# Attention block on one core: the two v of a pair made alternately in two PSUM banks

## The reference

```python
h = group_norm(x, scale, bias)                      # 32 groups
q, k, v = split(h @ qkv_w + qkv_b, 3, axis=-1)
q, k, v = (a.reshape(batch * 8, 1024, 64) for a in (q, k, v))
weight = softmax(einsum('btc,bsc->bts', q / 64**.25, k / 64**.25))
a = einsum('bts,bsc->btc', weight, v).reshape(batch, 1024, 512)
out = x + a @ proj_w + proj_b
```

## Time and profile before

| | |
|---|---|
| median of three runs | 3357.51 us |
| the profiled execution | 3357.48 us |
| its span, first to last instruction | 3355.7 us |
| PE busy | 3289.6 us, 98% |
| DVE busy | 2895.4 us, 86% |
| ACT busy | 2010.0 us, 60% |
| POOL busy | 1656.2 us, 49% |
| mean granted clock of PE | 0.997 |

### The profile page before, as it was taken

How to read it: one execution, slowest core, us unless ns; L and a number is a source line. 1 busy time by engine, 2 the same in 40 slices (tenths; PEclk the granted TensorE clock), 3 DMA queues, 4 the chain that set the end, 5 groups by cost and what they waited for, 6 DMA issues and landing times.

```text
span 3355.7 us, 66951 instructions
## 1 busy us (share of the span) xinstructions
PE 3289.6 (98%) x24128; PEld 2483.9 (74%) x24128; DVE 2895.4 (86%) x3601; ACT 2010.0 (60%) x3857; POOL 1656.2 (49%) x2762
## 2 busy tenths in 40 slices
PE   4999999999999999999999999999999999999998
PEld 4777777777777777777777777777777777777775
DVE  6888888888888888888888888888888888888886
ACT  4665665665665656656656666566566566565663
POOL 3454554554545544545545455445455454554452
PEclk9999999999999999999999999999999999999999
DMA  5888888888878888888888787878888788887777
GB/s 124 197 195 196 198 193 196 194 198 192 199 195 196 195 195 197 196 193 197 196 193 198 193 199 190 199 196 196 196 194 198 191 198 195 198 193 189 185 190 179
DMA packets 312633, 646.84 MB, mean 193 GB/s; under 512 B 80624, under 2 KB 146160, under 8 KB 312304
## 3 DMA queue, kind: packets, MB, share of 16 engines
q1 hardware_dynamic: 270784, 573.87, 72.6%
q10 hardware_dynamic: 41520, 68.71, 7.2%
HBM read 71.84 MB, written 33.55 MB: 31 GB/s over the span
## 4 chain that ended last, share of the span: by engine, by line
PE 94%; DVE 2%; SPq 1%; ACT 1%; DMA 0%; POOL 0%; issue 0%; ACTq 0%; POOLq 0%
PE pv_ps L372 25%; PE s_ps L343 23%; PE c_ps L408 7%; PE c_ps L409 7%; PE c_ps L410 7%; PE c_ps L422 4%; PE c_ps L424 3%; PE c_ps L423 3%; PE c_ps L390 3%; PE c_ps L391 3%; PE c_ps L392 3%; PE pv_ps L354 3%; DVE turned L624 1%; SPq L314 1%; ACT probs L465 1%; DVE neg_max L641 1%
## 5 line engine op out<-in xcount | busy, mean ns | idle before, releaser
L465 ACT ACTIVATE probs<-s_ps,neg_max 128x1024 f32<-128x1024 f32 x1024 | 1140.9, 1115 | 790.5 <-DVE neg_max L641 787.4
L641 DVE TENSOR_REDUCE neg_max<-s_ps 128x1 f32<-128x1024 f32 x1024 | 1205.1, 1219 | 257.2 <-PE s_ps L343 257.2
L624 DVE STREAM_TRANSPOSE turned<-probs 128x1024 f32<-128x1024 f32 x1024 | 1233.6, 1229 | 88.6 <-ACT probs L465 69.3
L372 PE MATMUL pv_ps<-probs_t,v 128*64 128x256 f32 x8192 | 943.0, 383 | 5.6 <-DMA probs_t<-turned 5.6
L372 PEld LDWEIGHTS pv_ps<-probs_t,v 128*64 128x64 f32 x8192 | 566.8, 137 | 357.3 <-issue 99.3
L408 PE MATMUL c_ps<-h_hi,w_hi 128*128 128x256 f32 x2048 | 592.0, 289 | 12.8 <-POOL h_lo L765 8.0
L485 ACT ACTIVATE staged<-c_ps,qk_bias 64x256 f32<-64x256 f32 x1024 | 480.9, 470 | 179.2 <-PE c_ps L410 165.9
L409 PE MATMUL c_ps<-h_lo,w_hi 128*128 128x256 f32 x2048 | 580.2, 283 | 0.0
L410 PE MATMUL c_ps<-h_hi,w_lo 128*128 128x256 f32 x2048 | 579.5, 283 | 0.0
L814 POOL COPY inv_wide<-inv_sum 128x256 f32<-128x256 f32 x256 | 102.1, 399 | 884.4 <-PE pv_ps L354 874.7
L408 PEld LDWEIGHTS c_ps<-h_hi,w_hi 128*128 128x128 f32 x2048 | 392.8, 192 | 18.4 <-issue 7.5
(11 more groups left out here) (68 smaller groups left out, 4946.9 us busy)
## 6 DMA issues: line engine op xcount, KB each, us to landing
probs_t<-turned SPq DMA_DIRECT2D x4096, 128.0 KB, 2.5
x_res<-in_x ACTq DMA_DIRECT2D x128, 256.0 KB, 3.6
result<-x_res ACTq DMA_DIRECT2D x128, 256.0 KB, 2.9
x_next<-in_x SPq DMA_DIRECT2D x480, 64.0 KB, 2.1
probs_t<-in_L_conv_qkv_w SPq DMA_DIRECT2D x48, 64.0 KB, 6.1
turned<-in_x SPq DMA_DIRECT2D x8, 128.0 KB, 6.1
turned<-in_x ACTq DMA_DIRECT2D x8, 128.0 KB, 6.4
probs_t<-in_L_conv_proj_w SPq DMA_DIRECT2D x4, 256.0 KB, 3.4
```

The lines of the kernel that those rows point to most:

```text
L372: last = nc.tensor.matmul(pv_ps[side][CH * par:CH * (par + 1), 0, :], v_sb[:, ring_of(i, parity), CH * chunk:CH * (chunk + 1)], p_t[:, par ...
L465: nc.scalar.activation(probs[k % 2][:, :], s_ps[k % 2][:, :], ACT.Exp, bias=neg_max[:, k % 4:k % 4 + 1], accum_out=row_sum[:, (k // HALF) ...
L624: nc.vector.transpose(dst, probs[k % 2][:, :].rearrange("p (k b j) -> p k b j", k=CHUNKS, b=QUADS)).then_inc(probs_turned, 1)
L641: nc.vector.tensor_reduce(neg_max[:, k % 4:k % 4 + 1], s_ps[k % 2][:, :], AX.X, ALU.max, negate=True).then_inc(max_ready, 1)
```

## The change

The two calls of `make_v` become one piece of work. The call for n = 0 waits for both banks and makes both v; the call for n = 1 returns at once. For each tile of channels and each of the three products it issues the matmul of the first block into c_ps0 and then that of the second block into c_ps1. The number of matmuls, their sizes and their operands stay, as do the sums' order within each bank. v_full is counted at the last matmul of each bank, which now are the last two of the 24.

```diff
             def make_v(b, k, i, n):
-                if not within(attended_pair(b, k), N_PAIRS):
-                    return
-                c = bank(k, i)
-                if attended_pair(b, k) == 0 and n == 0:
+                if n == 1 or not within(attended_pair(b, k), N_PAIRS):
+                    return
+                banks = [bank(k, 0), bank(k, 1)]
+                if attended_pair(b, k) == 0:
                     pe.wait_ge(w_ready, 3)
-                await_bank(pe, b, k, i)
+                await_bank(pe, b, k, 0)
+                await_bank(pe, b, k, 1)
                 for t in range(KT):
-                    hh, hl = (h[:, t, n * P:(n + 1) * P] for h in (h_hi, h_lo))
-                    nc.tensor.matmul(c[:, :], hh, w_hi[:, t, 2 * C:3 * C], start=(t == 0), stop=False)
-                    nc.tensor.matmul(c[:, :], hh, w_lo[:, t, 2 * C:3 * C], start=False, stop=False)
-                    last = nc.tensor.matmul(c[:, :], hl, w_hi[:, t, 2 * C:3 * C], start=False, stop=(t == KT - 1))
-                last.then_inc(v_full, 1)
+                    for h, w in ((h_hi, w_hi), (h_hi, w_lo), (h_lo, w_hi)):
+                        first, final = t == 0 and h is h_hi and w is w_hi, t == KT - 1 and h is h_lo
+                        for m, c in enumerate(banks):
+                            last = nc.tensor.matmul(c[:, :], h[:, t, m * P:(m + 1) * P], w[:, t, 2 * C:3 * C],
+                                                    start=first, stop=final)
+                            if final:
+                                last.then_inc(v_full, 1)
```

## The result

The changed kernel takes 3380.9 us in the median of four runs (3380.05 to 3382.21), against 3357.98 before (four runs, 3355.78 to 3359.09): 22.9 us slower, a ratio of 1.007 with a 95% interval of 1.0055 to 1.0085. The forecast was 3398, with a range of 3380 to 3414. The time lies 0.9 us inside its lower end: the way and the place are right, the loss is little more than half of the forecast one.

A forecast was written before the change was run, and what follows sets the result against it. PE's work, busy 98%, was taken as the bound; matmul pace unchanged, 62 x 0.62 = 38.4 us of stall plus the ends, together 40 us on 3357.48, gave 3398 us, range 3380 to 3414.

The forecast's parts named there:

- PE's own work at nothing: PE's 24 matmuls per pair: alternating banks costs and brings nothing; bounds 3 us of gain, 8 us of loss.
- The faster pace of 216 ns: Matmuls of v, rival: alternating makes them faster, stall stays; 3395 by traced paces, 3381 by the skill's figure; 6%.
- The first v 2.49 us later, DVE standing still: DVE's first taking of v: starts at 1546.87, not 1544.38; idle before takings rises from 55.8 to some 160 us.
- The wait at the second q/k tile of step 4: PE waits there for `take_proj` to empty c_ps0: 0.62 us in each of 62 pairs, 38.4 us; nothing carried on.
- A release of 0.05 us and a restart of 0.10: PE at that tile: starts 0.05 us after the bank is free; second matmul follows after 0.22, not 0.12.
- The delay of `take_proj`, 1.01 us at its end: DVE's taking of the projection: ends at 1558.72 instead of 1557.71, costing PE 0.62 us a pair.
- the sum of distances along DVE's queue: DVE, first v to `take_proj`: start distances 0.60, 1.21, 0.60, then 4.93 and 3.82 us, the last without idle time.
- The ends, 1.7 us: First and last pair: DVE's 1.28 us pass on in full in the first, say 0.4 in the last.
- Idle time before the q/k tiles, some 25 us more: Sign in the profile: PE's idle sum before the tile's first matmul rises by some 62 x 0.4 us, releaser `take_proj`.
- rival 1: Before the q/k tile, 0.54 us of room holds a delay under 0.49: 3359 us, 5%; with faster pace 3356 or less, 2%.
- the whole delay: Rival 3: step 4's scores wait for late exponentials, or DVE does not catch up; PE loses 1.28 us a pair, 3438, 8%.
- Rotating banks so that a taking overlaps the next product's matmuls: Skill's rule, at the two v: giving up the overlap costs one taking, 0.69 us x 62 = 43 us, or 3400.

The follow-up runs named there:

- 18 and with 24 alternations: Changed kernel with its last six matmuls in sequence, 3359.13 us; changed kernel with DVE's two takings of v behind the second transposition, 3358.03 us.
- the count at the 22nd: Kernel before, no alternation, with v_full of the first v counted only at the 22nd of the 24 matmuls: 3365.41 us, ratio 1.0021.
- one matmul more: Kernel before, no alternation, with DVE taking the first v only when both are counted, at the 24th matmul: 3395.97 us, ratio 1.011.

## Why the prediction was right, and where it was off

- *PE's own work at nothing*: right. 5.12 us for the same 22 distances, and 62 pairs of unchanged length with 18 and with 24 alternations. The faster pace of 216 ns that the Trainium skill gives ("TensorE: Matmul & The Clock Gate", "Back-to-back issue gap") for an isolated matmul did not come.
- *The first v 2.49 us later, DVE standing still*: right, 2.48 in the row, 152.4 us in all where 160 were forecast. In eight pairs the transposition ahead waits 0.2 to 1.2 us for the moves of earlier probabilities, and the wait for v is shorter by as much.
- *The wait at the second q/k tile of step 4, for the projection's bank, in 62 pairs, and nothing carried on*: right, shown by the releaser and by the run that takes the projection first.
- *A release of 0.05 us and a restart of 0.10*: right. 1567.95 + 0.65 is 1568.60, the tile starts at 1568.65 and its second matmul 0.23 later.
- *The delay of `take_proj`, 1.01 us at its end*: wrong in size, 0.72 in the rows (it ended 0.54 us ahead of the tile's place before, and ends 0.18 behind it after), and with it the 0.62 a pair. From the first taking of v to that end I had 11.85 us; the row after has 1568.60 - 1557.04 = 11.56, which is 0.29 less and the whole difference of 0.62 to 0.33. It was shorter nearly everywhere: transposition to taking 1.16 for 1.21, second taking to `largest` 0.57 for 0.60, from there to the `largest` of step 4 4.84 for 4.93, on to `take_proj` 3.73 for 3.82, and `take_proj` itself 0.65 for 0.69; only the first taking to the transposition is as said (0.61).
- *The step that failed* is the sum of distances along DVE's queue, and in it first the sentence that from the `largest` of step 4 to the taking of the projection there was no idle time. The row shows none, but the taking starts at 1557.02, and the projection's last matmul, the first row below, ends at 1556.98: 0.04 before, the same distance as from v's last matmul to its taking. DVE was waiting for PE there just as its transposition ended, and I took the distance of 1.21, and the same one for the taking of v, for DVE's own; without a wait it is 1.16, so 0.05 in each. In the change the projection's last matmul (the second row below) ends 0.80 us ahead of the taking.

```profile
1556.59 0.39 PE L392 MATMUL c_ps<-pw_hi,attn_lo 128*128 128x512 f32 x1
```

```profile
1566.76 0.39 PE L392 MATMUL c_ps<-pw_hi,attn_lo 128*128 128x512 f32 x1
```

Another 0.09 is, but for 0.01, my reading of the idle time: consecutive rows of DVE overlap by some 0.08 us, so a wait that is shown as 0.27 takes 0.35 out of the distance. The instruction ahead of the `largest` of step 4 starts 0.41 us before it in the kernel before (`largest` at 1553.20) and 0.06 after the change (at 1564.22):

```profile
1552.79 0.14 DVE L631 RECIPROCAL inv_sum<-row_sum 128x4 f32<-128x4 f32 x1
```

```profile
1564.16 0.14 DVE L635 RECIPROCAL inv_sum<-row_sum 128x4 f32<-128x4 f32 x1
```

The last 0.10 is that instructions behind a wait take longer than those that follow on work.
- *That the time lies in the range* is in part luck. The range had 8 us below for a shorter chain on DVE; the chain was shorter by 0.29 us x 62 = 18 us. The time stayed inside because the range also had room for a shorter restart and a faster pace, 9 us, and neither came.
- *The ends, 1.7 us*: 2.5 in the profile, 1.0 in front (1.28 forecast) and 1.5 behind (0.4).
- *Idle time before the q/k tiles, some 25 us more*: 4.1 us on PE (16.9 for 12.8) and 16.7 on the weight loads, by their new releaser, since the stall is smaller and the previous matmul still counts as busy for most of it.
- *The rivals*: the room of 0.54 us in front of the bank did not hold the delay, `take_proj` ending at 1568.60 where the tile would have started at 1568.30 + 0.12; with two matmuls less it holds it. The room was also smaller than the 0.49 that rival 1 has: with the count at the 22nd, `take_proj` is 0.48 us late and each pair still loses 0.10, since the tile's first weights are loaded 0.12 us ahead of its matmul. The scores of step 4 did not wait for the exponentials in the change, with the second slot's ending 1562.96 ahead of scores at 1563.16; with one matmul more they do. DVE had caught up by step 6, so the whole delay never reached PE.
- *Rotating banks so that a taking overlaps the next product's matmuls*, as the Trainium skill asks ("Perfetto Trace Analysis", "Optimizing Tensor Performance"): by this rule alone I had reckoned one taking a pair, 43 us. For the two v the runs show that giving it up costs nothing by itself (a ratio of 0.9999 with both takings at the end of both v). It costs what DVE's queue makes of it.

The rows for the scores of step 4 in the change, the end of the second slot's exponentials and the start of the scores that need it, 0.20 us apart:

```profile
1562.77 0.19 ACT L469 ACTIVATION_READ_ACCUMULATOR probs<-s_ps,neg_max 128x1 f32 x1
```

```profile
1563.16 0.39 PE L343 MATMUL s_ps<-kh,qh_o 64*128 64x512 f32 x2
```

## What to carry to other kernels

Before two results are made side by side, look at what the engine that takes them has queued behind the first: an in-order queue passes the wait on to work that has nothing to do with it, and the price is what that exceeds the room at the next shared buffer by. Here such a delay was free up to the room, and what went beyond it cost its full length; the same edit with the first v two matmuls earlier cost nothing. If the edit is wanted, move independent work ahead of the late taking; and where a chain is to be priced, take its distances from rows in which no input arrived just before the start.

## What the runs showed that was not expected

- An instruction of DVE that follows directly on another takes less than the same one behind a wait: the taking of 512 columns 0.65 and not 0.69 us, with the next start 0.57 and not 0.61 later; two `largest` 2.32 to 2.34 and not 2.36. On the way from the first v to the projection's bank this was worth 0.10 us a pair.
- PE can lose time with no idle time in its rows. With the count at the 22nd matmul each pair lost 0.10 us because a weight load was held that otherwise runs under the previous matmul. Only the distance of the next two starts, 0.22 for 0.12, shows it.
- Matmuls that alternate between two banks run at the pace of those that stay in one, to 0.01 us in 5.12; over 62 pairs, in the two kernels without a stall, to 0.01 us in 3181.80.
